# Attention scores of two heads as 64-row matmuls on the two halves of the array, in three rounds

## The chip, the cores and the metric

The kernel runs on one core of one Trainium2 chip. The metric is the device time of one execution in microseconds, the median of several runs. All data are 32-bit floats.

## The reference

Four blocks follow each other on x of shape (8, 512, 256), each as `x = x + layernorm(block(layernorm(x)))`:

```
L0 attention: 16 heads of 64, causal, with a bias slope(h) * (i - j)
    scores = q @ k.T * 64**-0.5 + bias;  attn = softmax(scores);  out = attn @ v;  out @ Wo + bo
L0 ffn:       x @ weight.T + pooled @ disha      (two products)
L1 attention: linear, two key/value states of 16 heads, product of the states, layernorm, Wo
L1 ffn:       64 experts, top 8 of each of the 4096 tokens by a softmax gate, plus a shared expert
```

The change is in the first line: for each batch of 512 tokens and each head, scores of 512 by 512 with a contraction over 64, masked to the lower triangle, and the softmax over them.

## The kernel before, in words

The program is written by hand for each engine: every engine has its own list of instructions in program order, and semaphores join them. There is no planner; what stands first in an engine's list is done first.

**Stages.** (1) Attention of batch 0 alone. (2) A loop of seven iterations: the attention of batch b+1, with the post work of batch b (everything after the first attention's values up to the routing of its tokens to experts) cut into 18 points (`post`, points 0 to 17) and placed between the pairs of heads. (3) The post work of batch 7 with the shared expert of the first four batches. (4) The 64 experts. (5) The shared expert of the last four batches and the final sums. The change touches stages 1 and 2.

**One batch of attention.** x is normalised by DVE (`x_norm`), transposed by PE, copied by ACT (`enter`). Values are made in eight units of 512 columns, six in `enter`, two after the scores of the first pair (`first_scores`); unit 6 waits for the first eight score tiles to be read. The 16 heads go in 8 pairs. Queries and keys of a pair are one product each of 128 rows (two heads of 64) by 512, both through bank 2: PE writes the queries (L1174), ACT copies them to `qT` with the scale (L541, `q_evac`), then PE writes the keys (L1180), and DVE copies them (`k_evac`, L756 to L759). In `kpad` each head has its own 128-row copy of the keys in which the rows of the other head are zero (cleared once by POOL, L442), so that a score matmul contracts over all 128 rows with the queries of both heads as its weights and gives the scores of one head.

**Scores.** A head has four tiles of 128 queries, t = 0 to 3, with 128, 256, 384 and 512 keys. `head_scores` (L1183) makes them in three units in banks 0, 1 and 3: tile 3; tiles 2 and 0; tile 1. A bank is used again by the next head once DVE has read it (`biased`). `pair_scores` (L1200) is: scores of head A, queries of the next pair, scores of head B, keys of the next pair. DVE reads each tile out of the bank, subtracts the distances with the mask and takes the row's maximum (`bias_and_max`, L761, matmul output to `prob`), four tiles of a head in a row and then their negated maxima (`negmax`, L776), for which ACT waits. `heads` (L782) is DVE's order: head A, post point 2.5 (in pair 2 alone), head B, k copy, reciprocals of head A.

**Behind the scores.** ACT takes the exponentials of both heads of a pair (`exps`, L556, four each, with the row's sum). DVE takes the reciprocals of the sums (L780), POOL multiplies (`normalise`, L472), PE transposes the probabilities (`pair_transposes`, L1209, three units a head in banks 4, 5, 2), ACT copies them to `pT` (`probs_out`, L565), PE multiplies with the values (`pair_values`, L1229, bank 3, the two heads on the two column halves of the array), ACT copies `oT`.

**Order.** PE does the scores of pair hp+1, then post point 2hp+1, then transposes and values of pair hp, then post point 2hp+2 (points 3 and 15 stand between transposes and values). ACT's list for the same stretch (`pair`, L572) has both heads' exponentials of pair hp+1 first and then the six copies of pair hp's transposes:

```
def pair(i, hp):
    for s in range(2):
        if hp + 1 < HP:
            exps(i, 2 * hp + 2 + s)
    for s in range(2):
        probs_out(i, 2 * hp + s)
```

DVE's is: `heads` of pair hp+1, post point 2hp+1, reciprocals of head B, post point 2hp+2. The third unit of the transposes uses bank 2 and so waits until DVE has copied the keys of the next pair but one (`k_ready`). PE's post work in a loop batch, by the pair whose scores it follows: pair 1 point 1 (L1250), pair 2 point 3 (L1263) and 4 (L1284), pair 3 points 5 and 6 (L1295, L1298), pair 4 points 7 (L1305) and 8 (L1313), pair 5 points 9 (L1250) and 10 (L1263), pair 6 point 11 (L1250), pair 7 points 15 and 16, and after it 17, the output product and the next batch's `enter`.

## Time and profile before

| | |
|---|---|
| median of 3 runs | 2499.14 us (2496.32 to 2499.89) |
| span of the profiled execution | 2494.8 us |
| around the span (median less span) | 4.3 us |
| mean granted TensorE clock | 0.966 |
| PE, DVE, ACT, POOL busy | 2304.8, 1177.7, 814.3, 836.6 us |
| attention of batch 0 | about 20 to 179 us |
| seven loop iterations | 179 to 1478 us |
| busy in the iteration from 548.20 to 735.12 | PE 169.32, DVE 114.46, ACT 81.27, POOL 76.59 us |

The profiled execution's own time is its span and the few microseconds around it.
### The profile page before, as it was taken

The page shows a single profiled execution, that of the slowest core. Times are in us where ns is not written, and L with a number is a line of the kernel's source. Part 1 is how long each engine was busy: PE and PEld are TensorE (multiplying, and loading weights), DVE is VectorE, ACT ScalarE, POOL GpSimd, SP SyncE. Part 2 cuts the span into 40 slices and gives each one's busy share as a digit, 9 for nine tenths or more (in the row PEclk, how much of TensorE's full clock was granted, in tenths as well). Part 3 has the DMA queues.
Part 4 walks back from the last instruction along what each step waited for, and adds up shares of the span by engine and source line. Part 5 has one row for each costly group of instructions (what it writes and reads, how often), then busy time and mean ns, then how long its engine had stood idle before and what let it go on. Part 6 is the DMA issues. An engine that isn't in the chain of part 4 may idle for free.

```text
span 2494.8 us, 38620 instructions
## 1 busy us (share of the span) xinstructions
PE 2304.8 (92%) x11988; PEld 1694.1 (68%) x11988; DVE 1177.7 (47%) x4191; ACT 814.3 (33%) x2104; POOL 836.6 (34%) x952
## 2 busy tenths in 40 slices
PE   7998988988998998998998989889999999999997
PEld 3555655655655655555555656579999999999854
DVE  3455665665655655655755752412222222222246
ACT  3634434534534534534534511111111111111110
POOL 3317417417407407417317350322222222222200
PEclk9999989999999999999999999989999999999999
DMA  9100002001001000000000040058777777777522
GB/s 324 58 1 18 1 18 76 8 17 40 9 9 34 9 9 23 9 12 24 9 13 17 9 161 17 12 182 255 238 250 246 237 256 237 249 247 236 169 93 93
DMA packets 99385, 244.79 MB, mean 98 GB/s; under 512 B 20532, under 2 KB 76051, under 8 KB 90976
## 3 DMA queue, kind: packets, MB, share of 16 engines
q1 hardware_dynamic: 73184, 224.34, 25.5%
q0 software_dynamic: 26112, 19.55, 4.8%
q14 instruction: 69, 0.57, 0.1%
q8 instruction: 20, 0.33, 0.1%
HBM read 194.23 MB, written 87.91 MB: 113 GB/s over the span
## 4 chain that ended last, share of the span: by engine, by line
PE 79%; DVE 13%; issue 4%; ACT 2%; DMA 1%; DVEq 0%; SPq 0%; ACTq 0%
PE bank L1456 17%; PE bank L1469 9%; PE bank L1196 8%; PE bank L1250 6%; PE bank L1397 6%; PE bank L1160 5%; PE bank L1240 5%; PE bank L1174 4%; PE bank L1180 4%; PE bank L1406 3%; PE bank L1224 3%; DVE stats L707 2%; PE bank L1263 2%; ACT prob L562 1%; DVE newton L721 1%
## 5 line engine op out<-in xcount | busy, mean ns | idle before, releaser
L478 POOL TENSOR_TENSOR prob<-prob,rsum 128x128 f32<-128x128 f32 (+3 forms) x512 | 360.9, 736 | 778.1 <-ACT prob L562 664.2
L1456 PE MATMUL bank<-pT,big_w 128*128 128x160 f32 x3072 | 440.6, 300 | 0.7 <-DVE pT L1041 0.7
L1456 PEld LDWEIGHTS bank<-pT,big_w 128*128 128x128 f32 x3072 | 425.0, 191 | 1.5 <-issue 0.8
L524 POOL DMA_INDIRECT acc<-qT,token_e x128 | 184.4, 1440 | 545.9 <-ACT qT L677 475.1
L770 DVE CUSTOM_DVE_ANT_0 prob<-bank,dist 128x512 f32<-128x512 f32 (+3 forms) x512 | 229.4, 488 | 287.9 <-PE bank L1196 285.3
L483 POOL DMA_INDIRECT disp<-send,slot x288 | 282.9, 982 | 198.7 <-DVE slot L971 113.9
L1196 PE MATMUL bank<-kpad,qT 128*128 128x512 f32 (+3 forms) x1024 | 300.6, 437 | 13.6 <-DVE rawmax L770 13.6
L562 ACT ACTIVATE prob<-prob,negmax 128x512 f32<-128x512 f32 (+3 forms) x512 | 280.4, 550 | 90.2 <-DVE negmax L776 90.2
L1196 PEld LDWEIGHTS bank<-kpad,qT 128*128 128x128 f32 x1024 | 170.0, 190 | 153.7 <-issue 77.8
L1224 PE MATMUL bank<-ident,prob 128*128 128x128 f32 x1280 | 181.7, 291 | 60.8 <-ACT pT L536 36.9
L670 ACT ACTIVATE pT<-bank 128x480 f32<-128x480 f32 x128 | 73.0, 570 | 496.5 <-PE bank L1456 496.5
L1469 PE MATMUL bank<-pT,big_w 128*128 128x160 f32 x1536 | 225.6, 303 | 0.0
L1224 PEld LDWEIGHTS bank<-ident,prob 128*128 128x128 f32 x1280 | 150.8, 148 | 95.7 <-ACT pT L536 46.6
L1469 PEld LDWEIGHTS bank<-pT,big_w 128*128 128x128 f32 x1536 | 210.3, 190 | 2.6
L536 ACT ACTIVATE pT<-bank 128x512 f32<-128x512 f32 (+1 forms) x384 | 174.1, 522 | 62.3 <-PE bank L1224 61.7
L1240 PE MATMUL bank<-pT,v_s 128*64 128x512 f32 (+3 forms) x1024 | 169.2, 476 | 0.9
L1056 DVE TENSOR_TENSOR pT<-pT,bank 128x480 f32<-128x480 f32 x128 | 83.7, 654 | 172.7 <-PE bank L1456 163.1
L1174 PE MATMUL bank<-xT,big_w 128*128 128x512 f32 x256 | 133.1, 646 | 6.6 <-ACT xT L536 6.6
L1240 PEld LDWEIGHTS bank<-pT,v_s 128*64 128x64 f32 x1024 | 69.8, 148 | 85.3 <-issue 58.1
L1063 DVE COPY gram<-bank 128x160 f32<-128x160 f32 x128 | 35.6, 320 | 189.4 <-PE bank L1469 189.4
L1180 PE MATMUL bank<-xT,big_w 128*128 128x512 f32 x256 | 120.3, 592 | 0.0
L1250 PE MATMUL bank<-big_w,oT 128*128 128x256 f32 x512 | 114.1, 381 | 5.9 <-DVE key L958 5.9
(177 smaller groups left out, 2781.2 us busy)
## 6 DMA issues: line engine op xcount, KB each, us to landing
big_w<-ew SPq DMA_DIRECT2D x64, 1536.0 KB, 7.1
big_w<-ew SPq DMA_DIRECT2D x64, 768.0 KB, 6.0
disp<-send SPq DMA_DIRECT2D x1, 10272.0 KB, 33.7
xT<-disp SPq DMA_DIRECT2D x64, 160.5 KB
disp<-send,slot POOLq DMA_INDIRECT x288
xs<-x SPq DMA_DIRECT2D x8, 512.0 KB, 4.3
x<-x SPq DMA_DIRECT2D x8, 512.0 KB, 3.6
x_d<-x SPq DMA_DIRECT2D x8, 512.0 KB, 2.6
```

The lines of the kernel that those rows point to most:

```text
L478: i = g.tensor_tensor(pr, pr, rsum[:, n, t:t + 1].to_broadcast([P, COLS[t]]), ALU.mult)
L483: g.indirect_dma_start(out=disp, out_offset=bass.IndirectOffsetOnAxis(ap=slot[:, t, k:k + 1], axis=0), in_=send[:, t, :], in_offset=None, ...
L562: a.activation(prob[:, n % 4, at_t], prob[:, n % 4, at_t], ACT.Exp, bias=negmax[:, n, t:t + 1], scale=slope(n), accum_out=psumm[:, n, t:t ...
L770: v.tensor_tensor_reduce(out=prob[:, n % 4, P_AT[t]:P_AT[t] + COLS[t]], in0=bank[S_BANKS[u]][:, col:col + COLS[t]], in1=dist[:, N - COLS[t ...
L1174: ins = mm(bank[2][:], wq_s[:, c, hp * P:(hp + 1) * P], xT[:, c], start=(c == 0), stop=(c == C - 1))
L1180: ins = mm(bank[2][:], wk_s[:, c, hp * P:(hp + 1) * P], xT[:, c], start=(c == 0), stop=(c == C - 1))
L1196: ins = mm(bank[S_BANKS[u]][:, col:col + COLS[t]], qT[:, hp % 2, t * P:(t + 1) * P], kpad[:, hp % 2, s, 0:COLS[t]], start=True, stop=True, ...
L1224: ins = nc.tensor.transpose(bank[T_BANKS[u]][:, col + (t - j) * P:col + (t - j + 1) * P], prob[:, (2 * hp + s) % 4, P_AT[t] + j * P:P_AT[t ...
L1240: ins = mm(bank[3][s * DH:(s + 1) * DH, j * P:N], v_s[:, j, (2 * hp + s) * DH:(2 * hp + s + 1) * DH], pT[:, s, T_AT[j]:T_AT[j] + N - j * P ...
L1250: ins = mm(bank[PA + t // 2][:, (t % 2) * D:(t % 2 + 1) * D], lhs[:, c, t * P:(t + 1) * P], rhs(c), start=(c == 0), stop=(c == chunks - 1) ...
L1456: i = mm(bank[2 * half + 1 - part][:, q * CAP:(q + 1) * CAP], w1[:, c, f * P:(f + 1) * P], xbT[:, c], start=(c == 0), stop=(c == C - 1), s ...
L1469: i = mm(bank[(4, 7)[c]][:, 0:CAP], w2[:, f, c * P:(c + 1) * P], act_e[:, f], start=(f == 0), stop=(f == FC - 1), skip_group_check=True)
```

## The change

The keys are kept unpadded in `kT` (both heads of a pair on their 64 rows, one copy by DVE for the pair instead of two, and no clearing by POOL). A score matmul contracts over 64 rows: head A on rows 0 to 63 of the array, head B on rows 64 to 127. The tiles of a pair go in three rounds: tile 3 of both heads in banks 0 and 1; tiles 2 and 0 of both heads in banks 3 and 0; tile 1 of both heads in banks 1 and 3. Between rounds 0 and 1 PE makes the next queries, between rounds 1 and 2 the next keys. DVE follows the rounds, copies the keys between rounds 1 and 2, and negates the maxima of both heads after round 2. Post point 2.5 follows the rounds. Semaphore counts are adapted.

```diff
--- before.py
+++ after.py
@@ -113,7 +113,7 @@
         xTp = sb("xTp", [P, C, N])
         v_s = sb("v_s", [P, T, INNER])
         qT = sb("qT", [P, 2, N])
-        kpad = sb("kpad", [P, 2, 2, N])
+        kT = sb("kT", [P, 2, N])
         qscale = sb("qscale", [P, HP])
         prob = sb("prob", [P, 2 * 2, 10 * P])
         rawmax = sb("rawmax", [P, H, T])
@@ -242,7 +242,6 @@
         POINTS = 2 * HP + 2
         PA, PB = 6, 7
         V_BANKS = 3, 4
-        S_BANKS = 0, 1, 3
         T_BANKS = 4, 5, 2
         V_FIRST = 6
 
@@ -254,7 +253,10 @@
         taken.append(len(steps) - sum(taken))
         UNITS = [steps[sum(taken[:n]):sum(taken[:n + 1])] for n in range(POINTS)]
         COLS = [(t + 1) * P for t in range(T)]
-        S_UNITS = [[(3, 0)], [(2, 0), (0, 3 * P)], [(1, 0)]]
+        S_ROUNDS = [[(3, 0)], [(2, 0), (0, 3 * P)], [(1, 0)]]
+        S_BANKS = [(0, 1), (3, 0), (1, 3)]
+        S_FREED = [(-2, -1), (1, 1), (2, 4)]
+        S_OPS = 2 * T
         P_AT = {3: 0, 2: 512, 0: 896, 1: 1024}
         T_UNITS = [[(0, 0)], [(1, 0), (3, 384)], [(2, 0)]]
         T_AT = {0: 0, 1: 512, 3: 896, 2: 1024}
@@ -265,7 +267,7 @@
 
         N_POST = 12 + 4 * KS
         N_ZEROS = 2 + LATE + 2
-        N_MADE = 18
+        N_MADE = 17
 
 
         @block.sync
@@ -439,7 +441,6 @@
             g.memset(blocks[:], 2.0 ** -20 * (1024.0 / L1N) ** 2).then_inc(setup_made, 1)
             g.memset(tri[:], 1.0).then_inc(setup_made, 1)
             g.memset(cum[:], 0.0).then_inc(setup_made, 1)
-            g.memset(kpad[:], 0.0).then_inc(setup_made, 1)
             g.memset(xn[:], 1.0).then_inc(setup_made, 1)
             g.memset(y[:], 0.0).then_inc(setup_made, 1)
 
@@ -755,38 +756,39 @@
 
             def k_evac(i, hp):
                 dve.wait_ge(k_psum, at(i, HP, hp + 1))
-                v.tensor_copy(kpad[0:DH, hp % 2, 0], bank[2][0:DH, :]).then_inc(k_ready, 1)
-                v.tensor_copy(kpad[DH:P, hp % 2, 1], bank[2][DH:P, :]).then_inc(k_ready, 1)
-
-            def bias_and_max(i, n):
-
-                if n >= 4:
+                v.tensor_copy(kT[:, hp % 2], bank[2][:]).then_inc(k_ready, 1)
+
+            def bias_and_max(i, hp, r, s):
+
+                n = 2 * hp + s
+                if r == 0 and n >= 4:
 
                     dve.wait_ge(pT_psum, at(i, 3 * H, 3 * (n - 3)))
-                for u, unit in enumerate(S_UNITS):
-                    dve.wait_ge(scores, at(i, 3 * H, 3 * n + u + 1))
-                    fixed()
-                    for t, col in unit:
-                        v.tensor_tensor_reduce(
-                            out=prob[:, n % 4, P_AT[t]:P_AT[t] + COLS[t]],
-                            in0=bank[S_BANKS[u]][:, col:col + COLS[t]], in1=dist[:, N - COLS[t]:N],
-                            scale=1.0, scalar=LOWEST, op0=ALU.subtract, op1=ALU.max,
-                            accum_out=rawmax[:, n, t:t + 1]).then_inc(biased, 1)
-                dve.wait_ge(biased, at(i, H * T, (n + 1) * T))
-                v.tensor_scalar(negmax[:, n], rawmax[:, n], -slope(n), None, ALU.mult).then_inc(max_ready, 1)
+                dve.wait_ge(scores, at(i, 3 * H, 6 * hp + 2 * r + s + 1))
+                fixed()
+                for t, col in S_ROUNDS[r]:
+                    v.tensor_tensor_reduce(
+                        out=prob[:, n % 4, P_AT[t]:P_AT[t] + COLS[t]],
+                        in0=bank[S_BANKS[r][s]][:, col:col + COLS[t]], in1=dist[:, N - COLS[t]:N],
+                        scale=1.0, scalar=LOWEST, op0=ALU.subtract, op1=ALU.max,
+                        accum_out=rawmax[:, n, t:t + 1]).then_inc(biased, 1)
+                if r == len(S_ROUNDS) - 1:
+                    dve.wait_ge(biased, at(i, H * T, hp * S_OPS + S_OPS - 1 + s))
+                    v.tensor_scalar(negmax[:, n], rawmax[:, n], -slope(n), None, ALU.mult).then_inc(max_ready, 1)
 
             def reciprocals(i, n):
                 dve.wait_ge(exped, at(i, H * T, (n + 1) * T))
                 v.reciprocal(rsum[:, n, :], psumm[:, n, :]).then_inc(rsum_ready, 1)
 
             def heads(i, hp, p=None):
-                bias_and_max(i, 2 * hp)
+                for r in range(len(S_ROUNDS)):
+                    if r == 2 and hp + 1 < HP:
+                        k_evac(i, hp + 1)
+                    for s in range(2):
+                        bias_and_max(i, hp, r, s)
                 if p is not None:
 
                     post(p, 2 * hp - 1.5)
-                bias_and_max(i, 2 * hp + 1)
-                if hp + 1 < HP:
-                    k_evac(i, hp + 1)
                 reciprocals(i, 2 * hp)
 
 
@@ -1169,7 +1171,7 @@
 
             def queries(i, hp):
                 if hp:
-                    pe.wait_ge(k_ready, at(i, 2 * HP, 2 * hp))
+                    pe.wait_ge(k_ready, at(i, HP, hp))
                 for c in range(C):
                     ins = mm(bank[2][:], wq_s[:, c, hp * P:(hp + 1) * P], xT[:, c], start=(c == 0), stop=(c == C - 1))
                 ins.then_inc(q_psum, 1)
@@ -1180,31 +1182,34 @@
                     ins = mm(bank[2][:], wk_s[:, c, hp * P:(hp + 1) * P], xT[:, c], start=(c == 0), stop=(c == C - 1))
                 ins.then_inc(k_psum, 1)
 
-            def head_scores(i, n):
-                hp, s = n // 2, n % 2
-                for u, unit in enumerate(S_UNITS):
-                    if n:
-
-                        pe.wait_ge(biased, at(i, H * T, (n - 1) * T + (1, 3, 4)[u]))
-                    if S_BANKS[u] == 3 and s == 0:
-
-                        if hp >= 2:
-                            pe.wait_ge(oT_ready, at(i, HP, hp - 1))
-                        else:
-                            pe.wait_ge(v_ready, at(i, 2 * T, 2 * T if hp else V_FIRST))
-                    for t, col in unit:
-                        ins = mm(bank[S_BANKS[u]][:, col:col + COLS[t]], qT[:, hp % 2, t * P:(t + 1) * P],
-                                 kpad[:, hp % 2, s, 0:COLS[t]], start=True, stop=True, skip_group_check=True)
-                    ins.then_inc(scores, 1)
+            def score_round(i, hp, r):
+
+                if r == 1:
+
+                    if hp >= 2:
+                        pe.wait_ge(oT_ready, at(i, HP, hp - 1))
+                    else:
+                        pe.wait_ge(v_ready, at(i, 2 * T, 2 * T if hp else V_FIRST))
+                for t, col in S_ROUNDS[r]:
+                    last_tile = (t, col) == S_ROUNDS[r][-1]
+                    for s in range(2):
+                        if (t, col) == S_ROUNDS[r][0] and (hp or r):
+                            pe.wait_ge(biased, at(i, H * T, hp * S_OPS + S_FREED[r][s]))
+                        rows = slice(s * DH, (s + 1) * DH)
+                        ins = mm(bank[S_BANKS[r][s]][:, col:col + COLS[t]], qT[rows, hp % 2, t * P:(t + 1) * P],
+                                 kT[rows, hp % 2, 0:COLS[t]], start=True, stop=True, skip_group_check=True)
+                        if last_tile:
+                            ins.then_inc(scores, 1)
 
             def pair_scores(i, hp):
-                pe.wait_ge(k_ready, at(i, 2 * HP, 2 * hp + 2))
-                head_scores(i, 2 * hp)
+                pe.wait_ge(k_ready, at(i, HP, hp + 1))
+                score_round(i, hp, 0)
                 if hp + 1 < HP:
                     queries(i, hp + 1)
-                head_scores(i, 2 * hp + 1)
+                score_round(i, hp, 1)
                 if hp + 1 < HP:
                     keys(i, hp + 1)
+                score_round(i, hp, 2)
 
             def pair_transposes(i, hp):
                 if hp == 0:
@@ -1218,7 +1223,7 @@
                             pe.wait_ge(pT_ready, at(i, 3 * H, m - 2))
                         if T_BANKS[u] == 2 and s == 0:
 
-                            pe.wait_ge(k_ready, at(i, 2 * HP, 2 * min(hp + 3, HP)))
+                            pe.wait_ge(k_ready, at(i, HP, min(hp + 3, HP)))
                         for j, col in unit:
                             for t in range(j, T):
                                 ins = nc.tensor.transpose(
```

## Rows read from the trace of the kernel before

**Rows 1.** The page, part 1: busy time, share and instructions of each engine.
```profile
PE 2304.8 (92%) x11988; PEld 1694.1 (68%) x11988; DVE 1177.7 (47%) x4191; ACT 814.3 (33%) x2104; POOL 836.6 (34%) x952
```

**Rows 2.** Timeline, PE, pair 4 of batch 0: start, us, engine, line, operation, idle before.
```profile
85.23 2.43 PE L1196 MATMUL bank<-kpad,qT 128*128 128x512 f32 x8
...
89.21 2.32 PE L1196 MATMUL bank<-kpad,qT 128*128 128x512 f32 x8
91.37 1.88 PE L1180 MATMUL bank<-xT,big_w 128*128 128x512 f32 x4
...
95.56 1.29 PE L1224 MATMUL bank<-ident,prob 128*128 128x128 f32 x10 [0.31 <-ACT pT L536]
96.97 2.37 PE L1240 MATMUL bank<-pT,v_s 128*64 128x512 f32 x16
99.28 0.70 PE L1196 MATMUL bank<-kpad,qT 128*128 128x512 f32 x1
```

**Rows 3.** Timeline, ACT, the same pair.
```profile
89.41 0.69 ACT L541 ACTIVATE qT<-bank,qscale 128x512 f32<-128x512 f32 x1 [3.48 <-PE bank L1174]
89.99 0.71 ACT L562 ACTIVATE prob<-prob,negmax 128x512 f32<-128x512 f32 x1
...
92.65 0.72 ACT L562 ACTIVATE prob<-prob,negmax 128x512 f32<-128x512 f32 x1 [0.38 <-DVE negmax L776]
...
94.84 2.75 ACT L536 ACTIVATE pT<-bank 128x512 f32<-128x512 f32 x6
```

**Rows 4.** Timeline, DVE, the same pair.
```profile
86.53 0.69 DVE L770 CUSTOM_DVE_ANT_0 prob<-bank,dist 128x512 f32<-128x512 f32 x1 [5.43 <-PE bank L1196]
...
88.11 0.42 DVE L770 CUSTOM_DVE_ANT_0 prob<-bank,dist 128x256 f32<-128x256 f32 x1
...
88.57 0.17 DVE L776 TENSOR_SCALAR negmax<-rawmax 128x4 f32<-128x4 f32 x1
...
93.28 0.68 DVE L758 COPY kpad<-bank 64x512 f32<-64x512 f32 x1 [0.67 <-PE bank L1180]
```

**Rows 5.** Timeline, PE, pairs 3 and 4 of batch 3.
```profile
604.83 2.32 PE L1196 MATMUL bank<-kpad,qT 128*128 128x512 f32 x8
...
612.58 1.89 PE L1295 MATMUL bank<-a_v,gram 128*128 128x256 f32 x8
614.31 1.03 PE L1298 MATMUL bank<-a_v,ssum_b 128*128 128x256 f32 x4
...
617.80 2.37 PE L1240 MATMUL bank<-pT,v_s 128*64 128x512 f32 x16
620.10 1.99 PE L1295 MATMUL bank<-a_v,gram 128*128 128x256 f32 x8
621.93 1.03 PE L1298 MATMUL bank<-a_v,ssum_b 128*128 128x256 f32 x4
622.80 2.32 PE L1196 MATMUL bank<-kpad,qT 128*128 128x512 f32 x8
...
630.55 1.95 PE L1305 MATMUL bank<-t,a_k 128*128 128x128 f32 x16
```

**Rows 6.** Waits, PE: line, waited for, us in total, times, longest.
```profile
PE bank L1224 <- ACT pT L536: 36.9, 21, 3.5
...
PE bank L1224 <- DVE kpad L759: 22.4, 13, 2.6
```

**Rows 7.** Timeline, PE, end of pair 5 of batch 3.
```profile
656.42 1.09 PE L1263 MATMUL bank<-ident,xn 128*128 128x128 f32 x8 [1.50 <-DVE xn L809]
```

**Rows 8.** Timeline, POOL, the start of the program.
```profile
2.17 1.80 POOL L442 MEMSET kpad<- 128x2048 f32 x1
```

**Rows 9.** Timeline, PE, pair 7 of batch 0.
```profile
136.00 1.92 PE L1224 MATMUL bank<-ident,prob 128*128 128x128 f32 x10 [2.96 <-ACT pT L536]
137.84 3.38 PE L1240 MATMUL bank<-pT,v_s 128*64 128x512 f32 x16
```

**Rows 10.** Windows, PE: stretch, its us, busy (instructions), granted clock, DMA share, GB/s.
```profile
136.00:141.30 5.30, 5.30 (x27) 0.68 0.01 3
```

## The prediction

> **What bounds the kernel now.** I read the page first, then the PE timeline of one pair of heads, then DVE and ACT in the same pair, then the pairs of the loop that carry more work, then the granted clock. Times within a pair are counted from S, the start of its first score matmul.
>
> PE is busy 92% of the span [rows 1], which suggests that a saved PE microsecond is a saved microsecond. In the attention of batch 0 that is nearly true and not quite. Pair 4 starts at 85.23, the next one at 99.28: a pair takes 14.05 us [rows 2]. Scores of head A, queries, scores of head B and keys follow each other without a gap up to S+7.85; then come the transposes of the pair before, the last ten of them at S+10.33 after a wait for ACT (pT). ACT's last exponential ends at 94.84, S+9.61 [rows 3], just where its copies out of the transposes' banks begin. So from the end of the exponentials to the last transposes are 0.72 us, and to the next pair 4.44 us. ACT must finish sixteen half-us operations (eight exponentials with their accumulator reads) before it may copy anything, since its program has both heads' exponentials ahead of the copies. Head A's four take 2.28 us back to back: they fill 89.99 to 92.27, and then ACT waits 0.38 for head B's maximum; head B's take 92.65 to 94.84, 2.2. Head A's maximum was ready at 88.74, S+3.51 [rows 4]. In short, PE and ACT are within a us of each other in these pairs, and **the time at which the maxima are ready** decides.
>
> In the loop (batches 1 to 7) post work of the batch before stands between scores and transposes. Pair 3 of batch 3 runs from 604.83 to 622.80 with 2.59 us of it ahead of the transposes (612.58 to 615.17) and 2.70 behind the values (620.10 to 622.80) [rows 5]: PE never waits there, it is the bound. Pair 4 has 1.78 us ahead (the 16 matmuls of L1305, without their tail). Pair 2 waits up to 2.6 for DVE's kpad [rows 6] and pair 5 ends on a 1.50 wait for DVE's xn [rows 7]: these are bound by DVE's post chain.
>
> **The change on PE.** Each score matmul is two passes. Eight passes of a head, 2560 columns, take 2.16 us (89.21 to 91.37) [rows 2]: 0.427 us for a pass of 512 columns, 0.32, 0.21 and 0.11 for 384, 256 and 128. The trace has no row-split matmul, but has the column-split ones of L1240: 16 passes on two halves, 5120 columns' worth, take 2.30 us (617.80 to 620.10) where one half alone would need 2.13 [rows 5]. The halves run wholly at once. I take the same for row halves: scores of a pair cost 2.13 instead of 4.32, saving 2.19. Bound on the other side: no overlap, saving 0.
>
> The mode changes cost. Leaving L1240 for full-array work, the first eight passes of L1295 take 1.83 us (620.10 to 621.93) where undisturbed they take 1.73 (612.58 to 614.31), and the values before end 0.1 later than their columns [rows 5]: 0.2 us a change. A pair now has six (in and out of each round, queries and keys between), one of which existed: +1.0 to 1.2. Bounds: 0, if the halves need no change, and 0.4 each.
>
> The Trainium skill (TensorEngine Tiling, Key Properties) says that changing the tiling mode, not just the tile, drains the array; it gives no price.
>
> The Trainium skill (TensorE: Matmul & The Clock Gate, Measured speedup vs the span model) has four row tiles reach 3.07 times instead of 4. Scaled to two halves that would be 1.54, an estimate from that page: 2.8 us of scores and some 12 us more in all. The column halves here show the full factor 2, so it isn't in the sum.
>
> New pair, in us from S: round 0 to 0.85; queries 1.05 to 2.76; round 1 2.96 to 3.81 (its bank needs head A's first tile read, which DVE has done by 1.9); keys 4.01 to 5.72 (they need q, which ACT has by 2.96 + 0.69 = 3.65 [rows 3]); round 2 5.92 to 6.35; next work at 6.55. Before it was 7.75. **PE gains 1.2 us a pair, if nobody is late.**
>
> **The change on DVE and ACT.** Both maxima now need round 2, behind the keys. The last key pass ends at 5.89 (its start and 0.59); the copy of k (0.68, once instead of twice) runs to 6.61; round 2 reaches DVE at 6.70, its last pass from 6.13 with 0.38 and the 0.19 that scores take to DVE; its 256-column tile and the negation took 0.63 (88.11 to 88.74) [rows 4]. Head A's maximum is ready at 7.33, where it was ready at 3.51; head B's follows 0.6 later, so ACT runs both heads' exponentials without a gap: 7.36 + 2.28 + 2.23 = **11.87, against 9.61**. ACT stands idle from the q copy to 7.36, the time in which it did head A before. The wait that vanishes (22.4 us in 13 waits for kpad [rows 6]; k is now there at 6.6) is replaced by one for pT: transposes of A are done at 7.7, those of B start at 11.87 + 0.72 = 12.6, the next pair at 11.87 + 4.44 = 16.3. POOL's normalising of these heads is needed only a pair later and stays covered. DVE's saved copy, 0.68 us, 64 times, lies inside that chain and is counted.
>
> The removed memset of 1.80 us [rows 8] lies under the weight loads that start PE; it lets the clearing transfers start 1.8 us earlier beside them, so 0 in the sum, +1.8 as a bound.
>
> **Sum.** Batch 0: pairs 1 to 6, 16.31 against 14.04, +2.27 each, 13.6. Pair 7 has no queries or keys; its rounds chain through DVE (read bank, next round), exponentials end at 9.9 against 7.9: +2.0. Pair 0: the value matmuls that wait for all eight tiles start 0.15 late. Together +15.8.
>
> A loop batch: pairs 0 to 2 +0.3 (0.15 as above; DVE's post chain sets the rest, and heads and k copy take it as long as before, since PE now waits for DVE between rounds). Pair 3: work up to the values' end was 15.27, now 16.31, +1.04. Pair 4, with 0.81 less post work ahead: +1.85. Pair 5, on DVE's chain: post work is fed earlier, but DVE must first take head A's reciprocal at 9.9, -0.6. Pairs 6 and 7 and what follows: PE's gain is lost to the exponentials, and pair 7's end 0.9 later: +0.9. Together +3.5, times seven 24.4.
>
> So far +40.2 us at full clock. Now the clock. In pair 7 of batch 0, PE waited 2.96 for ACT, and in the following 5.3 us the granted clock was 0.68 (part of them at 1.2 instead of 2.4 GHz) [rows 9, 10]. There the last transposes and values took 1.84 + 3.31 us, where at full clock they take 1.41 + 2.31: +1.4. The new idle stretch in batch 0's pairs is 12.6 - 7.7 = 4.9 us, longer than that one: 6 x 1.4 = 8.4. In pair 4 of the loop it is 3.1, about as long as that one: half of 7 x 1.4, 5. (Pair 3: 2.3, pairs 1 and 6: 1.3; I take nothing.) As an upper bound, twice the 1.4, 17 and 20.
>
> Sum +53.6: span 2494.8 + 53.6 = 2548.4. The runs lie 1.5 to 5.1 above that span, their median 4.3, so **2552.7 us** stands against the median 2499.1.
>
> **Rivals.** *A: the halves don't run at once* (the change does not do what it says). For it: no row-split pair is in the trace. Against: the column halves. The maxima come some 1.7 us later still, which 34 pairs feel (6 in batch 0; pairs 1, 3, 4, 6 in seven batches): +60 to 70, about 2617. Chance 0.12.
>
> *B: not slower: switches are free.* If consecutive rounds and full matmuls change over at no cost, PE is through at 5.55, and the maxima 0.8 earlier: exponentials end at 11.07, a pair in 15.5. Batch 0 still loses 1.47 x 6 and about 1.5. In the loop pair 0 gains 0.4, pair 1 0.6, pair 2 the k copy 0.7, pair 3 loses 0.24, pair 4 1.05, pair 5 gains 1.5, pair 6 0.6 and the rest 0.5: -3.0, times seven -21. Total -10, 2489. It decides at the change-over: below about 0.05 us each it is no slower. Against it stands the 0.2 of L1240 to L1295. Chance 0.08.
>
> *C: mild.* Chain as forecast, but the clock doesn't fall and half of the loop's loss hides under DVE: +15 to 25, 2515. Chance 0.05.
>
> **Numbers.** Forecast 0.75, by itself 2525 to 2590 (hot sum with no clock loss 2539, less 14 for cheaper change-overs; more clock loss and 0.4 per change at the top). The range, with C inside and part of A: 2512 to 2600. A measurement of this kernel tells about 0.2% (5 us) from no change. Faster by more than that 0.08 (B), within 0.04 (between B and C), slower 0.88.
>
> **What would show it.** The wait of L1224 for ACT's pT grows from 36.9 us in all [rows 6] to well over 100 (6 x 4.9 in batch 0, then 5.7, 2.3, 3.1, 4.2 and twice 1.4 a loop batch: near 150), and that for DVE's k copy goes. Starts of two score matmuls some ns apart show the halves at once; a first full-array pass 0.2 us late shows the change-over. Batch 0's pairs are 16 to 18 us apart. Last exponentials end near S+11.9. The mean granted clock falls below the 0.966 of now. Wrong would be: exponentials that end before S+10.5, or pairs of batch 0 below 14 us.

## The result, and the profile after

The changed kernel takes **2568.31 us** (median of 4 runs, 2566.51 to 2569.23), the kernel before 2499.05 in the runs beside it: ratio **1.028**, 95% interval 1.0265 to 1.0295. It is slower by 69 us. The forecast was 2552.7 with a range of 2512 to 2600.

The page of the changed kernel, parts 1 and the clock line of part 2:

```profile
span 2566.1 us, 38598 instructions
...
PE 2279.2 (89%) x11988; PEld 1617.5 (63%) x11988; DVE 1124.7 (44%) x4127; ACT 809.0 (32%) x2104; POOL 834.0 (33%) x951
...
PEclk9889999989989989989989989989999999999999
```

Against [rows 1] PE is busy 25.6 us less and the span is 71.3 us longer, at a mean granted clock of 0.944 instead of 0.966. A bound engine was relieved of work and the kernel got slower. The timeline of PE over one pair of batch 0 (start, us, engine, line, operation, idle before it) shows how; it answers to [rows 2]:

```profile
100.49 1.13 PE L1199 MATMUL bank<-kT,qT 64*128 64x512 f32 x4
101.55 1.98 PE L1176 MATMUL bank<-xT,big_w 128*128 128x512 f32 x4
103.47 1.14 PE L1199 MATMUL bank<-kT,qT 64*128 64x384 f32 x8
104.53 1.99 PE L1182 MATMUL bank<-xT,big_w 128*128 128x512 f32 x4
106.45 0.70 PE L1199 MATMUL bank<-kT,qT 64*128 64x256 f32 x4
107.08 1.31 PE L1229 MATMUL bank<-ident,prob 128*128 128x128 f32 x10
113.09 2.37 PE L1229 MATMUL bank<-ident,prob 128*128 128x128 f32 x10 [4.70 <-ACT pT L537]
115.39 4.19 PE L1245 MATMUL bank<-pT,v_s 128*64 128x512 f32 x16
119.51 0.70 PE L1199 MATMUL bank<-kT,qT 64*128 64x512 f32 x2
```

S, the start of the pair's first score matmul, is 100.49. Three short blocks of scores stand where two of 2.3 to 2.4 us stood, the next work starts at S+6.59, and then PE waits 4.70 us for ACT. What follows the wait is slow: ten transposes 2.37 and sixteen value matmuls 4.19 us, against 1.41 and 2.31 at full clock.

ACT in the same pair, for [rows 3]:

```profile
103.57 0.69 ACT L542 ACTIVATE qT<-bank,qscale 128x512 f32<-128x512 f32 x1 [2.36 <-PE bank L1176]
108.00 0.72 ACT L563 ACTIVATE prob<-prob,negmax 128x512 f32<-128x512 f32 x1 [3.74 <-DVE negmax L777]
...
110.20 0.70 ACT L563 ACTIVATE prob<-prob,negmax 128x512 f32<-128x512 f32 x1
...
112.38 1.32 ACT L537 ACTIVATE pT<-bank 128x512 f32<-128x512 f32 x3
```

ACT does nothing for 3.74 us and then runs both heads' exponentials without a gap, to S+11.89. DVE shows what ACT waits for, in answer to [rows 4]:

```profile
106.56 0.69 DVE L759 COPY kT<-bank 128x512 f32<-128x512 f32 x1 [0.30 <-PE bank L1182]
107.33 0.42 DVE L770 CUSTOM_DVE_ANT_0 prob<-bank,dist 128x256 f32<-128x256 f32 x1
...
107.80 0.17 DVE L777 TENSOR_SCALAR negmax<-rawmax 128x4 f32<-128x4 f32 x1
107.96 0.42 DVE L770 CUSTOM_DVE_ANT_0 prob<-bank,dist 128x256 f32<-128x256 f32 x1
...
108.43 0.17 DVE L777 TENSOR_SCALAR negmax<-rawmax 128x4 f32<-128x4 f32 x1
```

Head A's negated maximum is ready at S+7.48, behind the keys' product and their copy; before it was ready at S+3.51. The waits of PE, in answer to [rows 6] (total us, times, longest):

```profile
PE bank L1229 <- ACT pT L537: 149.3, 56, 4.7
...
PE bank L1199 <- DVE rawmax L770: 24.9, 23, 2.0
...
PE bank L1268 <- DVE xn L811: 19.5, 15, 6.8
PE bank L1162 <- DVE rawmax L770: 11.5, 8, 1.8
```

The wait for ACT grew from 36.9 to 149.3 us, and no wait for the keys' copy is left. In the loop the fifth pair of an iteration shows both losses. PE, pair 4 of batch 3, which starts at 668.74:

```profile
675.33 2.05 PE L1310 MATMUL bank<-t,a_k 128*128 128x128 f32 x16
677.22 1.25 PE L1229 MATMUL bank<-ident,prob 128*128 128x128 f32 x10
681.26 1.53 PE L1229 MATMUL bank<-ident,prob 128*128 128x128 f32 x10 [2.79 <-ACT pT L537]
682.72 3.84 PE L1245 MATMUL bank<-pT,v_s 128*64 128x512 f32 x16
```

A table of the time from one pair's first score matmul to the next one's, taken from the first starts of the score matmuls, says where the 71 us are:

| | pairs 0, 1, ... 7 (the last up to the next batch) | sum |
|---|---|---|
| batch 0, before | 11.18 13.94 14.05 14.04 14.05 14.04 14.04 51.31 | 146.65 |
| batch 0, after | 13.77 19.11 18.10 17.58 19.02 18.06 17.57 53.91 | 177.10 |
| batch 3, before | 12.06 16.14 28.43 17.97 15.91 18.64 16.14 61.63 | 186.92 |
| batch 3, after | 12.55 16.77 28.47 18.95 19.28 17.85 16.16 60.98 | 191.02 |

Batch 0 gives +30.5, the six iterations that follow it +34.5 together, the rest of the program +6.3. The six do not lose alike: four lose 4.1 to 4.8, the other two some 8.7, because two of the iterations before were 4.5 us shorter than the rest, mostly in pair 7 (58.0 and 58.1 instead of 61.2 to 61.8), and after the change none is. The clock goes with this: before, the mean granted clock was 0.972 in those two iterations and 0.936 in the other four; after the change it is 0.920 in all six.

### The profile page after: what moved, and what is told of

Same layout as the page of the kernel before. It is cut to its first block, busy times and chain, and to the rows that moved or that the text cites. A ratio compares the mean times of both kernels' runs of the same rounds, so it can differ in the third digit from the quotient of the medians.

```text
span 2566.1 us, 38598 instructions
## 1 busy us (share of the span) xinstructions
PE 2279.2 (89%) x11988; PEld 1617.5 (63%) x11988; DVE 1124.7 (44%) x4127; ACT 809.0 (32%) x2104; POOL 834.0 (33%) x951
## 4 chain that ended last, share of the span: by engine, by line
PE 76%; DVE 10%; ACT 7%; issue 6%; DMA 1%; DVEq 0%; SPq 0%; ACTq 0%
PE bank L1461 16%; PE bank L1474 9%; PE bank L1199 7%; PE bank L1245 6%; ACT prob L563 6%; PE bank L1402 6%; PE bank L1182 5%; PE bank L1176 5%; PE bank L1162 4%; PE bank L1229 4%; PE bank L1411 3%; PE bank L1255 3%; PE bank L1268 1%; DVE stats L708 1%; PE bank L1289 1%
## 5 line engine op out<-in xcount | busy, mean ns | idle before, releaser
L1229 PE MATMUL bank<-ident,prob 128*128 128x128 f32 x1280 | 196.9, 309 | 149.7 <-ACT pT L537 149.3
L1229 PEld LDWEIGHTS bank<-ident,prob 128*128 128x128 f32 x1280 | 163.1, 158 | 181.8 <-ACT pT L537 131.2
L1199 PE MATMUL bank<-kT,qT 64*128 64x512 f32 (+3 forms) x1024 | 194.6, 470 | 24.9 <-DVE rawmax L770 24.9
L1199 PEld LDWEIGHTS bank<-kT,qT 64*128 64x128 f32 x1024 | 85.2, 187 | 163.5 <-DVE rawmax L770 108.4
L1245 PE MATMUL bank<-pT,v_s 128*64 128x512 f32 (+3 forms) x1024 | 186.8, 514 | 0.1
L1176 PE MATMUL bank<-xT,big_w 128*128 128x512 f32 x256 | 139.5, 671 | 6.5 <-ACT xT L537 6.5
L1182 PE MATMUL bank<-xT,big_w 128*128 128x512 f32 x256 | 135.2, 654 | 0.0
L1162 PE MATMUL bank<-big_w,xT 128*128 128x512 f32 x256 | 117.2, 606 | 11.5 <-DVE rawmax L770 11.5
## 6 DMA issues: line engine op xcount, KB each, us to landing
disp<-send SPq DMA_DIRECT2D x1, 10272.0 KB, 34.5
```

The costliest lines, as they stand in the source:

```text
L1162: ins = mm(bank[V_BANKS[u % 2]][:], xT[:, c, (u // 2) * P:(u // 2 + 1) * P], wv_s[:, c, (u % 2) * 512:(u % 2 + 1) * 512], start=(c == 0), ...
L1176: ins = mm(bank[2][:], wq_s[:, c, hp * P:(hp + 1) * P], xT[:, c], start=(c == 0), stop=(c == C - 1))
L1182: ins = mm(bank[2][:], wk_s[:, c, hp * P:(hp + 1) * P], xT[:, c], start=(c == 0), stop=(c == C - 1))
L1199: ins = mm(bank[S_BANKS[r][s]][:, col:col + COLS[t]], qT[rows, hp % 2, t * P:(t + 1) * P], kT[rows, hp % 2, 0:COLS[t]], start=True, stop=T ...
L1229: ins = nc.tensor.transpose(bank[T_BANKS[u]][:, col + (t - j) * P:col + (t - j + 1) * P], prob[:, (2 * hp + s) % 4, P_AT[t] + j * P:P_AT[t ...
L1245: ins = mm(bank[3][s * DH:(s + 1) * DH, j * P:N], v_s[:, j, (2 * hp + s) * DH:(2 * hp + s + 1) * DH], pT[:, s, T_AT[j]:T_AT[j] + N - j * P ...
```

## The experiments

Each ratio is to the kernel before in runs on the same chip. "Order" stands for the order of ACT's list.

**1. ACT's copies between the two heads' exponentials.** If the late maxima hurt only because ACT's list has eight exponentials ahead of the copies, reordering the list should give the loss back.

```diff
-                for s in range(2):
-                    if hp + 1 < HP:
-                        exps(i, 2 * hp + 2 + s)
+                if hp + 1 < HP:
+                    exps(i, 2 * hp + 2)
                 for s in range(2):
                     probs_out(i, 2 * hp + s)
+                if hp + 1 < HP:
+                    exps(i, 2 * hp + 3)
```

> The changed kernel with ACT's order changed: exponentials of head A, then the six copies of the pair before's transposes, then exponentials of head B. Theory (the late maxima push ACT's sixteen exponential operations in front of the copies, PE waits for them and loses clock): the last ten transposes start near S+10.5 instead of S+12.6, pairs of batch 0 take about 14.1 instead of 18.2, pairs 1, 3, 4 and 6 of the loop 1 to 4 less; total 2475 to 2495, so below both kernels. Rival (what costs is PE's change between 64-row and full-array work): the changes are still all there, total stays within 5 of 2568.

Measured: 2523.0 us, ratio 1.0102 (1.0085 to 1.0119). The better part of the loss is gone, but it missed the forecast. PE in batch 0:

```profile
63.52 0.70 PE L1200 MATMUL bank<-kT,qT 64*128 64x256 f32 x4
64.15 1.31 PE L1230 MATMUL bank<-ident,prob 128*128 128x128 f32 x10
67.99 1.28 PE L1230 MATMUL bank<-ident,prob 128*128 128x128 f32 x10 [2.52 <-ACT pT L537]
69.39 2.37 PE L1246 MATMUL bank<-pT,v_s 128*64 128x512 f32 x16
71.70 1.13 PE L1200 MATMUL bank<-kT,qT 64*128 64x512 f32 x4
```

The wait is 2.52 instead of 4.70 and a pair 14.13 us, as forecast, where the clock holds (15.3 to 15.8 in three of pairs 1 to 6). What missed lies elsewhere. Pair 2 of an iteration takes 30.0 to 31.5 instead of 28.4: it ends on DVE's chain (PE's wait for `xn` is 47.4 us in 15 waits, 19.5 in the changed kernel), so the 1.7 us that pair 1 saves are waited away. And pair 7 takes 63 to 65 instead of 61 (here in batch 2, pair 7 from 499.14):

```profile
516.62 1.80 PE L1230 MATMUL bank<-ident,prob 128*128 128x128 f32 x10 [2.42 <-POOL prob L479]
518.97 1.91 PE L1269 MATMUL bank<-ident,send 128*128 128x128 f32 x8 [0.55 <-DVE send L812]
```

The last pair has no scores behind it to cover POOL's normalising. In batch 3 head B's exponentials end 4.3 us later in this pair than in the changed kernel and POOL's normalising 2.6 us later (S+17.4 instead of S+14.7), and PE waits for POOL 17.8 us in all.

**2. Control: the same order in the kernel before.**

> The kernel before with the same new order on ACT, as the control of e1. Theory: PE waits for ACT little there, and in batch 0 the transposes still wait for the k copy near S+9.5, so 2488 to 2499, 0 to 11 less than before. Rival (the order alone is worth what e1 gains, whatever the maxima): 2430 or less, 70 less than before.

Measured: 2509.44 us, ratio 1.0044 (1.0028 to 1.0061), slower and outside the forecast. Pairs of batch 0 shrink from 14.04 to 13.54, but pair 7's stretch grows to some 62.4 in five of six iterations and PE waits 20.0 us in all for POOL's `prob`. Most of the 12 us stand in the two iterations that had been short before (182.5 and 182.4, now 188.2 and 187.9). So the order is no improvement by itself that the change merely lacked: it repairs a wait that the change made.

**3. The three rounds with full-array matmuls.** This keeps the new order of the scores and takes the halves away, and with them the single copy of the keys: DVE copies twice again.

```diff
-                        rows = slice(s * DH, (s + 1) * DH)
-                        ins = mm(bank[S_BANKS[r][s]][:, col:col + COLS[t]], qT[rows, hp % 2, t * P:(t + 1) * P],
-                                 kT[rows, hp % 2, 0:COLS[t]], start=True, stop=True, skip_group_check=True)
+                        ins = mm(bank[S_BANKS[r][s]][:, col:col + COLS[t]], qT[:, hp % 2, t * P:(t + 1) * P],
+                                 kpad[:, hp % 2, s, 0:COLS[t]], start=True, stop=True, skip_group_check=True)
```

(and the padded copies of the keys as before)

> The changed kernel with the 64-row halves undone: padded keys, two k copies, full-array score matmuls, but the three rounds of the change in PE's and DVE's order. Theory (the rounds, not the halves, cost): scores end later, head A's maximum near S+9.1 and the exponentials near S+13.6, 1.7 after those of the change; total 2610 to 2650. Rival (the 64-row mode costs): back to 2500 to 2510.

Measured: 2653.25 us, ratio 1.0626 (1.0608 to 1.0644), just above the forecast. PE, one pair of batch 0 (its scores start at 87.08):

```profile
94.07 1.03 PE L1200 MATMUL bank<-kpad,qT 128*128 128x256 f32 x4
94.94 1.30 PE L1230 MATMUL bank<-ident,prob 128*128 128x128 f32 x10
101.47 2.37 PE L1230 MATMUL bank<-ident,prob 128*128 128x128 f32 x10 [5.23 <-ACT pT L538]
```

With the same order and slower scores the maxima come 1.8 us later still and a pair takes 20.5. **The rounds cost 156 us (against 2497.46 for the kernel before on that chip), and the halves with the single copy of the keys give some 85 of them back.** No run parts the halves from the copy.

**4. Halves, but head by head in the old order.** Head A's tiles all ahead of the queries, as before, each on 64 rows; no two halves run at once.

```diff
-                        ins = mm(bank[S_BANKS[u]][:, col:col + COLS[t]], qT[:, hp % 2, t * P:(t + 1) * P],
-                                 kpad[:, hp % 2, s, 0:COLS[t]], start=True, stop=True, skip_group_check=True)
+                        rows = slice(s * DH, (s + 1) * DH)
+                        ins = mm(bank[S_BANKS[u]][:, col:col + COLS[t]], qT[rows, hp % 2, t * P:(t + 1) * P],
+                                 kT[rows, hp % 2, 0:COLS[t]], start=True, stop=True, skip_group_check=True)
```

> The kernel before with 64-row matmuls on unpadded keys, but head by head in its old order (no two halves at once), one k copy. Theory: maxima as early as before (head A near S+3.5, the exponentials end near S+9.9), PE pays up to four changes of 0.2 a pair and saves nothing: 2510 to 2540. Rival (change-overs are most of the loss of 69 us): 2550 or more.

Measured: 2517.45 us, ratio 1.008 (1.0063 to 1.0097), as forecast. PE in batch 3:

```profile
588.49 2.42 PE L1195 MATMUL bank<-kT,qT 64*128 64x512 f32 x8
590.84 1.98 PE L1172 MATMUL bank<-xT,big_w 128*128 128x512 f32 x4
592.75 2.42 PE L1195 MATMUL bank<-kT,qT 64*128 64x512 f32 x8
595.10 1.99 PE L1178 MATMUL bank<-xT,big_w 128*128 128x512 f32 x4
```

Queries and keys after 64-row scores take 1.98 and 1.99 where the keys took 1.88 [rows 2], and scores after queries 2.42 where they took 2.32. In the PE-bound pairs this is +0.78 (pair 3: 18.75 against 17.97), four change-overs at **0.2 us each**. The 64-row mode by itself costs 20 us in all; the rounds are the loss.

**5. PE kept busy in the wait of batch 0.** Four products that nothing reads stand between the transposes of head A and of head B, in batch 0's pairs alone. This prices the clock.

```diff
+                    if s == 0:
+                        for _ in range(fill):
+                            mm(bank[PA][:], wq_s[:, 0, 0:P], xT[:, 0], start=True, stop=True)
```

> The changed kernel, with PE kept busy in batch 0: after the first ten transposes of pairs 0 to 6, four products nobody reads (8 passes of 512 columns, 3.4 us) into an unused bank, inside the 4.7 us in which PE waits for ACT. Theory (part of the loss is the clock, which falls after that idle time): granted clock 1 through batch 0, a pair takes 16.4 (S+11.9 plus 4.4) instead of 17.6 to 19.1, total 10 to 14 less than the change, 2555 to 2559, although PE does more. Rival (the wait alone costs, the clock nothing): same as the change, 2568, or more.

Measured: 2552.52 us, ratio 1.0215 (1.0198 to 1.0232), 16 us off the changed kernel, a little more than forecast. Two windows, from batch 0's first scores to batch 1's (us, then busy time of each engine, granted clock, DMA share, GB/s), first of the changed kernel:

```profile
31.94:209.04 177.10, 138.18 (x589) 75.85 (x589) 63.81 (x255) 74.48 (x206) 44.00 (x64) 0.87 0.25 75
```

and of this one:

```profile
31.55:193.42 161.87, 146.11 (x645) 77.45 (x644) 63.83 (x255) 73.66 (x206) 44.02 (x64) 1.00 0.28 83
```

More work in the same stretch, and it is 15.2 us shorter. The pairs stand at 16.31 and 16.32 us one after the other. So of batch 0's +30.5, half is the late maxima (161.87 less 146.65: 15.2) and half the clock (15.2). Not all of that clock is the filler's doing: 1.7 of it stands in pair 0, ahead of the first spare product, where the values behind a wait of 1.81 took 5.37 us in the changed kernel and 3.67 here. Pair 0 takes 12.07 in the traces of experiments 1 and 5 and 13.77 in those of the changed kernel and experiment 7, whatever the edit, so the filler is worth 13.5.

**6. Round 2 ahead of the keys.** All score rounds before the keys' product, and DVE copies the keys after the maxima.

```diff
                 score_round(i, hp, 1)
+                score_round(i, hp, 2)
                 if hp + 1 < HP:
                     keys(i, hp + 1)
-                score_round(i, hp, 2)
```

(and in DVE's `heads` the copy of the keys moves behind the loop over the rounds)

> The changed kernel with round 2 ahead of the keys on PE, and DVE's k copy behind round 2. Theory (the maxima's time decides): head A's maximum near S+6.2 instead of S+7.5, exponentials end near S+10.7; PE loses up to 0.9 a pair waiting for bank 3 between the rounds, which only pairs 5 and 0 feel; total 2515 to 2550. Rival (PE's own time decides): 0.9 a pair more, 2575 or above.

Measured: 2528.96 us, ratio 1.0117 (1.01 to 1.0134), as forecast. PE waits 0.59 for DVE between rounds 1 and 2, and the chain is earlier by more:

```profile
82.49 0.70 PE L1199 MATMUL bank<-kT,qT 64*128 64x256 f32 x2 [0.59 <-DVE rawmax L770]
83.11 1.98 PE L1182 MATMUL bank<-xT,big_w 128*128 128x512 f32 x4
84.94 1.45 PE L1229 MATMUL bank<-ident,prob 128*128 128x128 f32 x10
88.80 1.28 PE L1229 MATMUL bank<-ident,prob 128*128 128x128 f32 x10 [2.42 <-ACT pT L537]
```

Moving one block of 0.6 us ahead of a 1.9 us product, and the copy of the keys behind the maxima, brings 39 us: head A's maximum at S+6.31, the last exponential at S+10.72. The time of the maxima is a cause by itself, with ACT's list as it was.

**7. The new order everywhere but where pair 7's exponentials are made.** Experiment 1 with the old order for the last pair, so that POOL is not late.

```diff
+                late = hp + 2 == HP
                 if hp + 1 < HP:
                     exps(i, 2 * hp + 2)
+                    if late:
+                        exps(i, 2 * hp + 3)
                 for s in range(2):
                     probs_out(i, 2 * hp + s)
-                if hp + 1 < HP:
+                if hp + 1 < HP and not late:
                     exps(i, 2 * hp + 3)
```

> As e1, but for pair 7 ACT keeps the old order (both exponentials, then copies), because in e1 the span from pair 7 to the next batch grew from 61 to 63.4 to 64.7 us, with head B's exponentials ending at S+14.1 instead of S+9.8 and DVE's post chain behind them. Theory: that span returns to about 61, 2.5 to 3.5 less in each of seven iterations: 2495 to 2508. Rival (e1's growth is the clock's, by chance): 2520 to 2525.

Measured: 2501.69 us (10 runs), ratio 1.0008 (0.9998 to 1.0018), as forecast: nothing is left of the loss. Pair 7 takes 61.1 to 61.4 instead of 63 to 65 and no wait of PE for POOL is left, so the last pair was where experiment 1 lost. The equal time is a balance: pairs 1, 3, 4, 5 and 6 of an iteration are 0.4 to 1.1 us shorter each than in the kernel before, while pair 0 is 0.5 and pair 2 some 1.6 longer, batch 0 is 10.2 us longer (156.88 against 146.65), and the mean granted clock of the profiled executions is 0.950 against 0.966.

**8. Experiments 6 and 7 together.**

> Both of e6 and e7. Theory: nobody waits for the maxima any more; scores and keys end at S+7.7, as before the change, and the last transposes start near S+9.1, so the pairs are bound by PE as they were before: 2485 to 2505. Rival (the two gains are independent and add up): below 2470.

Measured: 2506.23 us (10 runs), ratio 1.0021 (1.001 to 1.0032), a little outside. Batch 0 gains (pairs of 12.97 us, its 143.34 us the shortest of all), but an iteration takes 187.7 where experiment 7 has 184.3: pairs 1, 3 and 6 lose 0.9 each, pair 7 1.0. The two remedies don't add up. In pair 3 PE now waits 0.59 between rounds 1 and 2 where it had waited for nothing; in all it waits 79 times, 65.3 us, for DVE to read a bank, against 23 times and 44.9 us in experiment 7.

**9 to 11. Versions with filler.** These three ran on another chip of the same kind, on which the kernel before takes 2541.93 us (9 runs), some 42 us more than on the chip of experiments 5 to 8; only ratios and differences on that chip are used. Experiment 9 is experiment 7 with spare products (nobody reads them) in the waits of batch 0, in pairs 2 and 7 of the loop and at the head of its batches (`FILL_R` is ahead of round 1 of the pair):

```diff
+        FILL0 = 2, 2, 2, 2, 2, 2, 3, 0
+        FILL = 0, 2, 0, 0, 0, 0, 2, 0
+        FILL3, FILLX, FILL_R = 4, 3, {2: 4, 7: 2}
...
+            def spare(b, n):
+                for _ in range(n):
+                    mm(bank[b][:], ident[:], dist[:], start=True, stop=True)
```

> e7 with products nobody reads (identity times distances, 0.86 us each) where its PE waits for 2 us and more: 2 or 3 between the transposes of the two heads in batch 0 and in pairs 2 and 7 of the loop, 4 and 2 ahead of round 1 in pairs 2 and 7, 4 ahead of post point 3, 3 ahead of the next batch's transposes. Theory (e7 ran 252 us at half clock against 173 before, and that is what is left of its loss): half-clock time below 120 us, total 2478 to 2492, below the kernel before. Rival (its clock does not matter, or the filler delays as much as it gives): 2498 to 2508.

Experiment 10 is the control: spare products in the kernel before, full-array scores in their old order.

> Control of e9: the kernel before with such products in its own waits (3 in pair 7, 2 and 1 in pair 2, 3 ahead of the next batch's transposes). Theory: 173 us at half clock fall to below 110; 2482 to 2494. Then e9 is no better than this one and the 64-row halves give nothing by themselves. Rival (the halves are worth the 1.2 us a pair that they save on PE once nobody waits): this one stays 10 or more above e9.

Experiment 11 takes from experiment 9 a wait of PE at the head of each batch, by giving value unit 6 a bank that no score round uses:

```diff
-                if u == V_FIRST:
-                    pe.wait_ge(biased, at(i, H * T, 2 * T))
                 for c in range(C):
-                    ins = mm(bank[V_BANKS[u % 2]][:], xT[:, c, (u // 2) * P:(u // 2 + 1) * P],
+                    ins = mm(bank[5 if u == V_FIRST else V_BANKS[u % 2]][:], xT[:, c, (u // 2) * P:(u // 2 + 1) * P],
```

(and ACT copies that unit out of bank 5)

> e9 with the seventh value unit in bank 5 instead of bank 3, so that PE does not wait 1.4 to 1.8 us in pair 0 for the last score tiles to be read (L1162 in the change: 11.5 us in 8 waits). Theory: batch 0 gains 1.4 to 1.8; in the loop pairs 0 to 2 are set by DVE's post chain and POOL and gain little: 2 to 8 less than e9. Rival (that wait is on the path in every batch): 11 less.

| | median us | ratio, interval | less than before | granted clock |
|---|---|---|---|---|
| 9, experiment 7 with filler | 2514.66 | 0.9896 (0.9881 to 0.9911) | 27.3 | 0.983 |
| 10, before with filler | 2505.70 | 0.9859 (0.9839 to 0.9879) | 36.2 | 0.983 |
| 11, experiment 9 with bank 5 | 2495.19 | 0.9816 (0.9802 to 0.983) | 46.7 | 0.982 |

The forecasts of 9 and 10 were made from 2500 us, and meant 8 to 22 and 6 to 18 us less than before; both gained more. Experiment 10 forecloses the easy reading of experiment 9: with the clock held up in both, the halves without the bank are 9 us behind the old scores. Experiment 11 beats both kernels, and the control by 10.5 us. The bank would bring the control nothing: its trace has no wait of PE ahead of value unit 6. But each kernel's filler was fitted to its own waits, and neither to the least time, so the 10.5 us hold for these two fillers. PE in batch 0 of experiment 11, where two spare products (L1224, two instructions each) leave 0.48 of the wait:

```profile
77.21 1.31 PE L1241 MATMUL bank<-ident,prob 128*128 128x128 f32 x10
78.58 1.98 PE L1224 MATMUL bank<-dist,ident 128*128 128x512 f32 x4
81.05 1.28 PE L1241 MATMUL bank<-ident,prob 128*128 128x128 f32 x10 [0.48 <-ACT pT L540]
82.45 2.37 PE L1263 MATMUL bank<-pT,v_s 128*64 128x512 f32 x16
84.76 1.13 PE L1207 MATMUL bank<-kT,qT 64*128 64x512 f32 x4
```

A pair takes 14.14 us. The gain of 11 over 9, 19.5 us, is larger than both forecasts. Their profiled executions differ by 8.9 (spans 2506.3 and 2497.4), and pair 0, whose wait was removed, is 1.46 shorter in each iteration (12.55 to 11.09), 10 in seven, of which other stretches give a little back; the profiled execution of 9 is the fastest of its five (2508.28) and that of 11 the slowest of its five (2499.33), so the traces cannot show where the rest of the difference of the medians lies.

## Why the prediction was right

The mechanism and most of its terms held; the sum fell 18 us short of the span (+53.6 forecast, +71.3 measured). By its steps:

- **Halves at once: right.** The trace has the first matmuls of heads A and B start 6 to 7 ns apart, and a pair's three blocks of scores hold PE for 2.75 us (1.06, 1.06, 0.63 from their start to that of the next work): 2.13 of columns and three change-overs. The gain of four row tiles that the Trainium skill gives (TensorE: Matmul & The Clock Gate, Measured speedup vs the span model), scaled to two halves, was an estimate of 1.54; the trace does not bear it out, two row halves of 32-bit data give the full 2. Rival A is out.
- **Change-over 0.2 us: right.** Four passes of queries take 1.98 instead of 1.88 and start some 0.1 later; experiment 4 gives 0.78 for four. The Trainium skill (TensorEngine Tiling, Key Properties) has the array drain at such a change; the trace agrees that the change costs time, 0.2 us, and does not show by what. Rival B is out.
- **The chain to the exponentials: right.** One row was misread on the way: ACT's "sixteen half-us operations" are eight exponentials of 0.39 to 0.72 us and eight reads of the accumulator of 0.19, but the 2.28 and 2.23 us for a head's four, which the sum uses, are right. And PE's start of the next work was S+7.85 in batch 0 before, 7.75 only where no change-over stands ahead, so PE gained 1.26 there rather than 1.2. Next work S+6.59 (6.55 forecast), head A's maximum S+7.48 (7.33), exponentials done S+11.89 (11.87), transposes of head B S+12.60 (12.6), the wait for pT 149.3 us (near 150). The late maxima by themselves cost batch 0 15.2 us (experiment 5) where +15.8 was forecast. Experiments 1, 3 and 6 change the maxima's time or what stands behind them, and the time follows each.
- **The clock in batch 0: the step that was mis-sized.** It was +1.4 a pair, 8.4 in all, taken from pair 7 [rows 9, 10]. It is 15.2: against experiment 5 pairs 1 to 6 lose 11.5, and pairs 0 and 7, for which nothing was taken, 1.7 and 2.0 (the 1.7 comes and goes with the execution, see experiment 5). The row that gave 1.4 stands behind a wait of 2.96; behind one of 4.70 transposes take 2.37 and values 4.19, where experiment 5 has 1.28 and 2.38.
- **The clock in pair 4 of the loop: half of the iterations was wrong.** It falls in every one: pair 4 stands at 19.27 to 19.33 in the six iterations, +3.4, which is the forecast +1.85 and some 1.5 of clock (5.23 us for transposes and values that take 3.72 at full clock). The wait is 2.79 where 3.1 was forecast. The window over 681.26 to 686.49:

```profile
681.26:686.49 5.23, 5.23 (x27) 2.44 (x27) 0.88 (x2) 2.05 (x5) 3.26 (x5) 0.67 0.00 0
```

- **Pairs 0 to 2: +0.3 forecast, +1.2 measured in batch 3.** The value unit that waits for eight tiles was put at 0.15; pair 0 alone is 0.49 longer. PE, first pair of batch 1:

```profile
217.08 3.70 PE L1162 MATMUL bank<-big_w,xT 128*128 128x512 f32 x8 [1.39 <-DVE rawmax L770]
```

The same place in the kernel before, whose batch 1 starts at 178.67:

```profile
186.42 3.60 PE L1160 MATMUL bank<-big_w,xT 128*128 128x512 f32 x8
189.85 1.04 PE L1263 MATMUL bank<-ident,xn 128*128 128x128 f32 x8
```

PE's saving of 1.2 us became a wait of 1.39, and the values start at S+8.04 instead of S+7.75: 0.29 where 0.15 was forecast. The change-overs ahead of the values (3.54 instead of 3.43 to the start of the transposes of `xn`) and ahead of the next scores (0.97 instead of 0.87) are the other 0.2 of the 0.49, and they had been left out. Pair 1 is 0.63 longer, for which nothing was taken although a wait of 1.3 was seen coming. It is 1.73 in batch 3 (for ACT's pT), more than PE had saved, and before there was none.
- **Pairs 3 and 5: right** (+0.98 for +1.04, -0.79 for -0.6). **Pairs 6, 7 and the rest: wrong in sign** in the four iterations that compare (-0.1 to -0.7 for +0.9), and too small in the other two, where pair 7 grew by 3.1 and pairs 0 to 2 by 1.9. In those two the kernel before had a granted clock of 0.972 where its other iterations had 0.936; after the change all six have 0.920. So the clock took more there than the forecast had; why it had held in just those two was not tested.

The clock, pairs 0 to 2 and pairs 6 and 7 make up the missing 18: batch 0 +6, the loop +9, the last batch and behind it +2.

Rival C, no fall of the clock and half of the loss hidden, is out by the 0.87 of batch 0.

## What to carry to other kernels

Time saved on the busiest engine counts only if the engines that it feeds get their inputs no later: here 1.2 us a pair were saved on PE, and the first maximum came 4 us later, because head A's last tile was moved behind two unrelated products and behind head B's tiles. Before interleaving two chains to share hardware, write down when each chain's first result is complete, and reorder the consumer's list along with the producer's. Waits of PE of 2.8 to 4.7 us cost twice in this kernel, as wait and as a low clock behind it (0.67 behind 2.79), so fill or close them before judging an edit, and run the filler on the kernel before too.

## What was not expected of the hardware

- **Filling pays.** With 56 more instructions on PE batch 0 took 15.2 us less, 13.5 of them behind the first filler, and spare products alone took 36.2 us off the kernel before (experiment 10), the same clock of 0.983 then standing in the page of both versions.
- **POOL holds back a small DVE operation.** A 128x4 tensor_scalar that takes 0.17 us (median of 72) took 3.31 beside POOL's normalising, and ended with it. DVE, then POOL, in the changed kernel:

```profile
617.09 3.31 DVE L714 TENSOR_SCALAR vare<-mv 128x4 f32<-128x4 f32 x1
```

```profile
617.62 2.75 POOL L479 TENSOR_TENSOR prob<-prob,rsum 128x128 f32<-128x128 f32 x4
```

It is in both kernels (2.5 to 2.7 us before), and in all seven iterations of both it ends within 0.04 us of the last of POOL's multiplications. It adds some 3 us to DVE's list in pair 1, and DVE's chain, not its busy time, bounds pairs 0 to 2; how much of the 3 us is on the path was not tested. That POOL is the cause was read from the rows, and no run took POOL's work away.
- **Two chips differ in one stage.** From the last batch's pair 7 to the first expert it is 221 to 225 us in the kernels before and after and in experiments 5 and 7, and 261 to 269 in experiments 9 to 11 on the other chip. From the first to the last of the 64 experts it is 701 to 702 us in all of them, and pairs of batch 0 in the control agree to 0.01 us with those of before (14.05). The plain kernel was not profiled on the other chip; its median is 42 us longer there.
